# A new hand-written order for every engine of an attention and FFN block kernel

## Chip, cores and metric

One Trainium2 chip, one core (eight are there, one is used). The metric is device time in microseconds (us) of one execution: the median of the runs shown.

## What is computed

Input x has 16 sequences of 512 rows with 256 features (fp32). The reference is

```python
x = x + _layernorm(attn(_layernorm(x)))     # 16 heads of 16, rope on q and k
x = x + _layernorm(ffn(_layernorm(x)))      # 256x256, both operands quantised to fp6 in blocks of 32
# inside attn, with h = layernorm(x) * ln_w + ln_b, q, k, v = h @ w_q, h @ w_kv:
qk = einsum('bhkd,bhqd->bhkq', rope(k), rope(q)) * scale
t = 1.0 + qk + 0.5 * qk * qk
wv = (t / sum(t)) @ v                        # a Taylor softmax, of degree 2
```

## The kernel before

The weights of a Taylor softmax are a polynomial of q and k, so attention is a product of features. A tile is 128 rows of one sequence (NT = 4 tiles a sequence, 64 in all). For each tile the stages are, by engine:

- **Input:** stats_x, moments_x, normalise_x (VectorE, L1326 to L1341) with add_x and rstd_x (GpSimd: an add of one column and a power); turn_z (TensorE transposes), copy_h, high_h (ScalarE), low_h (GpSimd, L1580): fp32 products are made of a high and a low part, three products each (split_product, L644 to L647).
- **q, k, v:** project_v, project_kq (TensorE), copy_v (ScalarE), rope_sin, rope_cos (VectorE, both read PSUM), rope_add (L1367, two SBUF inputs), extend_k (a copy).
- **Features:** products_1 and products_0 (VectorE, L540: products of k's parts, 128x672 and 128x896), products_2 (GpSimd, L540, 128x224), half_turn (GpSimd, L1597), square_k, high_q (ScalarE), low_q (GpSimd, L1585), turn_q (TensorE), copy_q. sum_features (TensorE, L873, 32 matmuls) sums them over a sequence.
- **Once a sequence:** copy_sums, turn_sums (L882), copy_main, rest_terms, constant, rest_matrix (L891, L895), copy_rest.
- **Attention:** select_0 to select_4 (TensorE, L689) with square_0 to square_4 (ScalarE, L1014, L1016), attend (TensorE, L752, L755), copy_quad (ScalarE). SyncE then moves the quad by eight small DMAs (move_quad: sums and heads_out). When a sequence's four quads are there, invert_sums (VectorE, L1405) takes the reciprocals of the denominators, SyncE spreads them by eight DMAs (spread_shares, L626), and normalise_attention (VectorE, L1421) multiplies. Every tile waits there for its own two of the eight. The last two sequences go through TensorE transposes instead (turn_quads, turn_attention).
- **Output of attention:** high_attention, low_attention (GpSimd, L1606), project_out, square_y, add_y, rstd_y, add_attention (VectorE, L1452, reads PSUM).
- **FFN:** centre, square_s (ScalarE), block_maxima, scales, inverse_scales, to_grid (L1470), from_grid (L1478), turn_ffn_input (TensorE), high_ffn_input, low_ffn_input (VectorE, reads PSUM), ffn, add_bias (VectorE, reads PSUM), square_f, add_f, rstd_f, add_ffn (VectorE, L1493), and the store.

Each engine runs its own list in order; semaphores tie the lists together. An instruction that waits holds up all behind it on its engine. The order is written by `stage_steps`: stage s of tile t is issued at step t + LAG[s], corrected by FIRST for the first 12 tiles and by FINAL for the last 16. Within one step the calls in the engine's `step(n)` give the order, so every step of the middle looks alike. `fill` and `drain` (L661) issue idle products of 128x128 with no use for the result: `warm_up` 12 at first, the fills 76 more (88 in all) while the first tiles pass, the drains 96 at the end.

## Time and profile before

| what | value |
|---|---|
| runs | 647.86, 649.33, 651.04 us |
| median | 649.33 us |
| the profiled execution | span 648.2 us; no time of its own is given apart from it |
| TensorE matmul | 624.1 us busy, 96% |
| VectorE | 605.9 us, 93% |
| ScalarE | 569.1 us, 88% |
| GpSimd | 464.6 us, 72% |
| TensorE weight loads | 471.8 us, 73% |
| granted TensorE clock, mean | 0.995 of full speed |
| chain of waits, by engine | VectorE 42%, TensorE 40%, issue 13%, the rest 5% |

PE is TensorE, PEld its weight loads, DVE VectorE, ACT ScalarE, POOL GpSimd, SP SyncE (with q: its queue). Busy time of TensorE is modelled: its matmuls are pipelined. A busy share is a mean over the run; the first 60 us and the last 80 us differ from the middle. In rows of windows the columns are the edges in us, the length, then busy us (instructions) of PE, PEld, DVE, ACT, POOL, the granted clock PEclk (1.00 is full speed), the DMA engines' share and GB/s.

### The profile page before, as it was taken

Reading aid. Unit: us, or ns where it says so; the run is one execution under the profiler, and the core shown is the slowest. Engines: PE = TensorE matmul, PEld = TensorE weight load, DVE = VectorE, ACT = ScalarE, POOL = GpSimd, SP = SyncE. Lnnn points to the kernel's source line nnn. Section 1 sums busy time; section 2 is a strip of 40 time slices with the busy share of each in tenths; the row PEclk is TensorE's granted clock in tenths of the full one; section 3 lists DMA queues with packets and bytes.
Section 4 is the critical chain, followed back from the end, with each engine's and each line's share of the span. In section 5 each row is a group of like instructions: output and inputs, shape, how many; then the busy total and the mean of one; then the engine's idle time right before and its main releaser. Section 6 shows DMA issues by size and latency. Waiting matters only on the chain.

```text
span 648.2 us, 20990 instructions
## 1 busy us (share of the span) xinstructions
PE 624.1 (96%) x6760; PEld 471.8 (73%) x6760; DVE 605.9 (93%) x1424; ACT 569.1 (88%) x1571; POOL 464.6 (72%) x842
## 2 busy tenths in 40 slices
PE   6889999999999999999999999999999999999998
PEld 6676767776777767777776777767767777778887
DVE  5989989999999999999999999999999999996696
ACT  3558899999998999999898999989899999999974
POOL 2675657797778777877787788777777877676364
PEclk9889999999999999999999999999999999999999
DMA  7101121222222232222322222222222212220111
...
DMA packets 52362, 43.54 MB, mean 67 GB/s; under 512 B 7200, under 2 KB 48544, under 8 KB 52256
## 3 DMA queue, kind: packets, MB, share of 16 engines
...
q10 hardware_dynamic: 816, 0.79, 0.4%
...
## 4 chain that ended last, share of the span: by engine, by line
DVE 42%; PE 40%; issue 13%; ACT 2%; POOL 2%; DMA 1%; DVEq 1%; SPq 0%; ACTq 0%; POOLq 0%
DVE kf L540 6%; PE ps_f L689 5%; PE ps_mt L873 5%; DVE xd L1478 4%; DVE kf L1367 4%; PE ps_o L752 4%; DVE z L1340 4%; PE ps_o L755 4%; DVE xs L1452 3%; PE ps_w L644 2%; DVE y L1470 2%; DVE fin L1493 2%; DVE t L1350 2%; DVE fb L1487 2%; PE ps_qk L644 2%
## 5 line engine op out<-in xcount | busy, mean ns | idle before, releaser
L1014 ACT ACTIVATE feat<-ps_f 128x512 f32<-128x512 f32 x256 | 153.1, 604 | 10.9 <-PE ps_f L689 10.2
L689 PE MATMUL ps_f<-qT,selr 128*128 128x512 f32 x320 | 138.0, 436 | 0.6 <-ACT feat L1014 0.6
L540 DVE TENSOR_TENSOR kf<-kf 128x672 f32<-128x672 f32 (+1 forms) x128 | 134.5, 1052 | 2.0
L873 PEld LDWEIGHTS ps_mt<-kf,vp 128*32 128x32 f32 x2048 | 65.5, 109 | 34.1 <-issue 33.3
L1612 POOL TENSOR_TENSOR ve_y<-var_y,epst 128x1 f32<-128x1 f32 x64 | 13.0, 204 | 104.6 <-ACT squares_y L1134 104.5
L873 PE MATMUL ps_mt<-kf,vp 128*32 128x153 f32 x2048 | 78.8, 293 | 0.4 <-ACT rm L1043 0.4
L689 PEld LDWEIGHTS ps_f<-qT,selr 128*128 128x128 f32 x320 | 60.0, 188 | 18.0 <-issue 14.9
L1580 POOL TENSOR_TENSOR hT_l<-hT,hT_h 128x256 fp32r<-128x256 f32 x63 | 56.0, 890 | 23.2 <-ACT hT_h L1079 23.2
L1068 ACT ACTIVATE hT<-ps_tr,small,lnwx 128x128 f32<-128x128 f32 x128 | 51.8, 456 | 20.6 <-PE ps_tr L726 20.5
L752 PE MATMUL ps_o<-feat,main 120*32 120x512 f32 x448 | 59.7, 604 | 0.0
L755 PE MATMUL ps_o<-feat,rm 128*32 128x512 f32 x448 | 58.9, 593 | 0.0
L1585 POOL TENSOR_TENSOR qsp<-kf,qsp 128x256 fp32r<-128x256 f32 x64 | 55.5, 867 | 1.8 <-ACT qsp L1123 1.8
L1606 POOL TENSOR_TENSOR attT_l<-att,attT_h 128x256 fp32r<-128x256 f32 x56 | 49.1, 877 | 9.0 <-ACT attT_h L1054 5.9
L540 POOL TENSOR_TENSOR kf<-kf 128x224 f32<-128x224 f32 x64 | 52.8, 825 | 3.8 <-DVE kf L1374 3.8
L1597 POOL TENSOR_TENSOR kf<-kf 128x128 f32<-128x128 f32 x64 | 53.9, 843 | 0.0
L644 PE MATMUL ps_qk<-wkqv_h,hT_l 128*128 128x512 f32 x126 | 53.9, 428 | 0.0
L645 PE MATMUL ps_qk<-wkqv_l,hT_h 128*128 128x512 f32 x126 | 50.5, 401 | 0.0
L1358 DVE TENSOR_TENSOR t<-ps_qk,sinT 128x512 f32<-128x512 f32 x64 | 43.7, 683 | 5.7 <-PE ps_qk L647 3.5
L1016 ACT ACTIVATE feat<-ps_f,small 128x512 f32<-128x512 f32 x64 | 44.2, 690 | 3.2 <-PE ps_f L689 2.8
L1367 DVE TENSOR_TENSOR kf<-t 128x512 f32<-128x512 f32 x64 | 45.4, 709 | 0.3
L1350 DVE TENSOR_TENSOR t<-ps_qk,cosT 128x512 f32<-128x512 f32 x64 | 42.2, 660 | 2.2 <-PE ps_qk L647 2.2
L1340 DVE TENSOR_SCALAR z<-xa,mv,rs_x 128x256 f32<-128x256 f32 x64 | 41.3, 645 | 2.2 <-POOL rs_x L1616 2.1
...
## 6 DMA issues: line engine op xcount, KB each, us to landing
...
heads_out<-osb SPq DMA_DIRECT2D x224, 32.0 KB, 2.0
shares<-sums SPq DMA_DIRECT2D x112, 64.0 KB
sums<-osb SPq DMA_DIRECT2D x224, 2.0 KB
...
xa<-L_attn_x SPq DMA_DIRECT2D x1, 384.0 KB, 5.5
```

The lines of the kernel that those rows point to most:

```text
L540: return eng.tensor_tensor(dims(row, F_MAIN, [[FW, heads], [HD, NR - 1], [1, HD]]), dims(row, F_LIN, [[FW, heads], [0, NR - 1], [1, HD]]), ...
L644: pe.matmul(out_, xl(c), wh(c), start=c == 0, stop=False)
L689: pe.matmul(ps_f[i % 2][:, :], selr[:, i], queries, start=True, stop=True).then_inc(sel_done, 1)
L752: pe.matmul(ps_o[VW * h:VW * (h + 1), :], main[0:NP, par, quad, VW * h:VW * (h + 1)], feat[0:NP, p2, h], start=True, stop=False, skip_grou ...
L755: mm = pe.matmul(ps_o[VW * h:VW * (h + 1), :], rm[:, par, quad, VW * h:VW * (h + 1)], feat[:, p2, HQ], start=False, stop=True, skip_group_ ...
L873: mm = pe.matmul(ps_mt[qd // 2][VW * h:VW * (h + 1), (qd % 2) * NF:(qd % 2 + 1) * NF], vp[:, s2, qd * HQ + h], kf[:, s2, qd * HQ + h, 0:NF ...
L1014: act.activation(feat[:, p2, i], ps_f[i % 2][:, :], ACT.Square).then_inc(squared, 1)
L1340: dve.tensor_scalar(z[:, t.two], xa[:, t.par, t.tile], mv[:, t.two, 0:1], rs["x"][:, t.two:t.two + 1], ALU.subtract, ALU.mult).then_inc(z_ ...
L1350: dve.tensor_tensor(t1[:].rearrange("p (h d) -> p h d", d=HD), ps_qk[:, :].rearrange("p (h d) -> p h d", d=HD), cos, ALU.mult).then_inc(qk ...
L1367: dve.tensor_tensor(dims(kf[:, t.two, 0, 0:1], F_LIN, [[F_Q - F_LIN, 2], [FW, H], [1, HD]]), t1[:].rearrange("p (a h d) -> p a h d", a=2, ...
L1580: pool.tensor_tensor(hT_l[:, p2], hT[:], hT_h[:, p2].bitcast(F32), ALU.subtract).then_inc(hT_low, 1)
L1585: pool.tensor_tensor(dims(qsp[:, p2], HQ * HD, [[2 * HQ * HD, NQ], [HD, HQ], [1, HD]]), dims(kf[:, p2, 0, 0:1], F_Q, [[HQ * FW, NQ], [FW, ...
```

## The change

The lags are replaced by ORDER: for every engine and stage, the places (slots of that engine's own list) of the first tiles, of a cycle of four tiles (one sequence) that repeats every `pitch` slots, and of the last tiles. TensorE has 58 slots a sequence, ScalarE 75, VectorE 79, GpSimd 52, SyncE 11. Stages once a sequence, of the last eight tiles, and the two loads of x have places of their own (RATE). IDLE is empty: no fill and no drain is issued, warm_up stays. Four waits are added that the new orders need (on s_squared, z_ready, rope_ready, xd_ready).

```diff
--- before.py
+++ after.py
-LAG = {
-    "warm_up": -20, "fill_a": 0, "sum_features": 3, "select_2": 7, "project_v": 1, "drain_b": 16, "select_3": 7,
-    "ffn": 16, "select_4": 7, "turn_q": 3, "turn_sums": 3, "turn_quads": 11, "project_kq": 1, "turn_z": 0,
-    "select_0": 6, "turn_ffn_weight": 7, "project_out": 13, "select_1": 6, "turn_ffn_input": 15, "rest_matrix": 3,
...
+TAIL = 2
+
+
+ORDER = {
+    "tensor": (58, {
+        "attend": ((41, 51, 63, 75, 89, 100, 112, 124, 138, 152, 167, 183, 196, 211, 225, 241, 255, 269, 283, 299, 313,
+            326,), (23, 37, 51, 67,), (676, 689, 705, 718, 733, 747, 763, 778, 791, 805, 821, 836, 850, 860, 875, 891,
+            901, 918, 924,)),
...
+    "vector": (79, {
+        "add_attention": ((142, 156, 167, 187, 209, 229, 250, 271, 290, 310, 334, 352, 370, 389, 409, 429, 450, 469,
+            489, 509, 528, 549, 573, 591, 610, 631, 651, 671, 691, 711, 731, 751, 768, 790, 809, 829, 847, 868, 886,
+            905, 924, 947, 961, 983, 1005, 1025, 1046, 1061, 1081, 1101, 1119, 1137, 1150, 1160, 1174, 1187, 1199, 1211,
+            1224, 1233, 1247, 1257, 1266, 1277,), (), ()),
...
+        "invert_sums": ((116, 166, 247,), (99,), (499, 576, 650, 724, 802, 883, 957, 1038, 1116,)),
...
+        "normalise_attention": ((121, 128, 136, 149, 176, 189, 206, 227, 255, 267, 292, 319, 342, 358, 378, 398, 423,
+            434, 456, 474, 508, 514, 532, 551, 584, 590, 608, 628, 656, 672, 689, 709, 736, 743, 761, 792, 815, 832,
+            852, 872, 894, 913, 935, 950, 973, 991, 1012, 1030, 1052, 1071, 1093, 1107, 1123, 1131, 1136, 1149, 1173,
+            1178, 1195, 1210, 1218, 1232, 1242, 1258,), (), ()),
+        "normalise_x": ((4, 9, 14, 25, 35, 45, 52, 61, 74, 84, 94, 103, 115, 125, 140, 152, 178, 196, 217, 238, 257,
...
+    "gpsimd": (52, {
...
+        "products_2": ((14, 16, 23, 29, 35, 42, 48, 53, 59, 64, 72, 80, 88, 100, 110, 123, 136, 145, 162, 171, 184, 197,
+            210, 224, 236, 249, 263, 277, 288, 301, 314, 331, 341, 352, 363, 378, 390, 402, 417, 428, 443, 454, 469,
+            481, 493, 506, 521, 532, 544, 560, 575, 589, 600, 613, 625, 636, 652, 664, 677, 690, 703, 715, 728, 740,),
+            (), ()),
...
-FIRST = {
-    "fill_a": (-18, -17, -20, -18, -23, -22, -25, -22, 0, 0, 0, 0),
-    "sum_features": (-19, -18, -18, -15, -11, -9, -6, -4, -3, -2, 0, 0),
...
-FINAL = {
-    "sum_features": (0, 0, 0, 0, 0, 0, 0, 0, 0, 0, 0, 0, 0, 3, 9, 13),
...
-EARLY, LATE = 12, 16
-TAIL = 2
-IDLE_FIRST, IDLE_LAST = 8, 12
-
-
-def stage_steps(count):
-
-    plan = {}
-    for stage, lag in LAG.items():
-        steps = plan.setdefault(stage, {})
-        for tile in range(count):
-            step = tile + lag
-            if tile < EARLY:
-                step += FIRST.get(stage, (0,) * EARLY)[tile]
-            elif tile >= count - LATE:
-                step += FINAL.get(stage, (0,) * LATE)[tile - count + LATE]
-            steps.setdefault(step, []).append(tile)
-    return plan
+RATE = {"angles": "once", "bias_mean": "once", "cast_identity": "once", "cast_selection": "once", "centre_bias": "once",
+RATE = {"angles": "once", "bias_mean": "once", "cast_identity": "once", "cast_selection": "once", "centre_bias": "once",
+    "constant": "sequence", "copy_ffn_weight": "once", "copy_main": "sequence", "copy_rest": "sequence", "copy_sums":
...
+IDLE = {"fill": (), "drain": ()}
+
+
+def places(table, count):
+
+    first, cycle, last, pitch = table
+    steps = {}
+    for index in range(count):
+        if index < len(first):
+            place = first[index]
+        elif index >= count - len(last):
+            place = last[index - count + len(last)]
+        else:
+            place = cycle[index % len(cycle)] + pitch * (index // len(cycle))
+        steps[place] = index
+    return steps
 
 
...
@@ -302,10 +424,15 @@
 def sandwich(nc, x, w_q, w_kv, w_o, weight, bias, identity, columns, selection, out):
     NS = x.shape[0]
     TILES = NS * NT
-
-
-    plan = stage_steps(TILES)
-    issued = {stage: 0 for stage in plan}
+    BODY = TILES - NT * TAIL
+    assert NT * TAIL == 8
+    counts = {"tile": TILES, "body": BODY, "tail": TILES - BODY, "sequence": NS, "spread": NS - TAIL, "load": NS - 2, "once": 1}
+
+    plan, issued = {}, {}
+    for engine, (pitch, tables) in ORDER.items():
+        for name, table in tables.items():
+            plan[name] = places(table + (pitch,), counts[RATE.get(name, "tile")])
+            issued[name] = 0
 
     class Tile:
 
@@ -318,42 +445,55 @@
 
     def each(n, name, stage, *args):
 
-        for index in plan[name].get(n, ()):
-            stage(Tile(index), *args)
+        if n in plan[name]:
+            stage(Tile(plan[name][n]), *args)
             issued[name] += 1
 
     def once(n, name, stage):
 
-        for index in plan[name].get(n, ()):
-            if index % NT == NT - 1:
-                stage(Tile(index))
+        if n in plan[name]:
+            index = plan[name][n]
+            stage(Tile(NT * index + NT - 1))
+
+    def body(n, name, stage):
+
+        each(n, name, stage)
+
+    def tail(n, name, stage):
+
+        if n in plan[name]:
+            stage(Tile(plan[name][n] + BODY))
+            issued[name] += 1
+
+    def spread(n, name, stage):
+
+        once(n, name, stage)
+
+    def load(n, name, stage):
+
+        if n in plan[name]:
+            index = plan[name][n]
+            stage(index + 2)
 
     def setup(n, name, stage):
 
-        if n == LAG[name]:
+        if n in plan[name]:
             stage()
 
-    def early(n, name, stage):
-
-        for index in plan[name].get(n, ()):
-            if index < IDLE_FIRST:
-                stage()
-
-    def late(n, name, stage):
-
-        for index in plan[name].get(n, ()):
-            if index >= TILES - IDLE_LAST:
-                stage()
+    def idle(n, name, stage):
+
+        for _ in range(IDLE[name].count(n)):
+            stage()
 
     def wait(eng, sem, count):
 
         if count > 0:
             eng.wait_ge(sem, count)
 
-    def every_step(step):
-
-        used = {n for steps in plan.values() for n in steps}
-        for n in range(min(used), max(used) + 1):
+    def every_step(engine, step):
+
+        last = max(n for name in ORDER[engine][1] for n in plan[name])
+        for n in range(last + 1):
             step(n)
 
     with ExitStack() as ctx:
...
             def step(n):
-                once(n, "invert_sums", spread_shares)
-                each(n, "move_quad", move_quad)
-                each(n, "add_ffn", store)
-                for seq in range(2, NS):
-
-                    if NT * (seq - 1) - 1 in plan["normalise_x"].get(n, ()):
-                        load_stream(seq)
-                    if NT * (seq - 1) - 1 in plan["add_attention"].get(n, ()):
-                        load_again(seq)
+                spread(n, "spread_shares", spread_shares)
+                body(n, "move_quad", move_quad)
+                each(n, "store", store)
+                load(n, "load_stream", load_stream)
+                load(n, "load_again", load_again)
 
             def store(t):
                 sp.wait_ge(fin_ready, t.n)
...
             def fill():
-
-                if issued["attend"] == 0:
-                    idle_products(ps_o, 2)
+                idle_products(ps_o, 2)
 
             def drain():
-
-                if issued["select_4"] == TILES:
-                    pe.wait_ge(squared, CHUNKS * TILES)
-                    idle_products(ps_f[1], 2)
+                pe.wait_ge(squared, CHUNKS * TILES)
+                idle_products(ps_f[1], 2)
 
             def select(t, i):
 
...
             def step(n):
+                idle(n, "fill", fill)
+                idle(n, "drain", drain)
                 setup(n, "warm_up", warm_up)
-                early(n, "fill_a", fill)
                 each(n, "sum_features", sum_features)
                 each(n, "select_2", select, 2)
                 each(n, "project_v", project_v)
-                late(n, "drain_b", drain)
                 each(n, "select_3", select, 3)
                 each(n, "ffn", ffn)
                 each(n, "select_4", select, 4)
                 each(n, "turn_q", turn_q)
                 once(n, "turn_sums", turn_sums)
-                each(n, "turn_quads", turn_quads)
+                tail(n, "turn_quads", turn_quads)
                 each(n, "project_kq", project_kq)
                 each(n, "turn_z", turn_z)
                 each(n, "select_0", select, 0)
...
@@ -1139,6 +1257,7 @@
                 act.wait_ge(xs_ready, t.n)
 
                 wait(act, y8_done, t.n - 2)
+                wait(act, s_squared, t.n - 2)
                 act.activation(c3[:, c2], xs[:, t.four], ACT.Identity, bias=ssum[:, c2:c2 + 1], scale=-float(D)).then_inc(centred, 1)
 
             def square_s(t):
@@ -1332,6 +1451,7 @@
 
             def moments_x(t):
                 dve.wait_ge(stats, t.n)
+                wait(dve, z_ready, t.n - 2)
                 dve.bn_aggr(mv[:, t.two], st[:, t.two]).then_inc(means, 1)
 
             def normalise_x(t):
@@ -1346,6 +1466,7 @@
                 cos = dims(cosT[:], t.tile * HD, [[0, 2 * H], [1, HD]])
                 if t.n == 1:
                     dve.wait_ge(tables_done, 1)
+                wait(dve, rope_ready, t.n - 1)
                 dve.wait_ge(qk_done, t.n)
                 dve.tensor_tensor(t1[:].rearrange("p (h d) -> p h d", d=HD), ps_qk[:, :].rearrange("p (h d) -> p h d", d=HD),
                                   cos, ALU.mult).then_inc(qk_read, 1)
@@ -1354,6 +1475,7 @@
                 sin = dims(sinT[:], t.tile * HD, [[0, 2 * H], [2, 8], [1, 2]])
                 if t.n == 1:
                     dve.wait_ge(tables_done, 1)
+                wait(dve, rope_ready, t.n - 1)
                 dve.wait_ge(qk_done, t.n)
                 dve.tensor_tensor(dims(t2[:], 0, [[HD, 2 * H], [2, 8], [1, 2]]), dims(ps_qk[:, :], 1, [[HD, 2 * H], [2, 8], [-1, 2]]),
                                   sin, ALU.mult).then_inc(qk_read, 1)
@@ -1459,6 +1575,7 @@
 
             def scales(t):
                 dve.wait_ge(amax_done, t.n)
+                wait(dve, xd_ready, t.n - 2)
                 dve.tensor_scalar(sc[:, t.two], amax[:, t.two], 2.0**6 / (D * FP6_MAX), SMALLEST, ALU.mult, ALU.max).then_inc(sc_done, 1)
 
             def inverse_scales(t):
```

In the middle of the run the tables come out as follows (the number is the tile, counted from a multiple of 4). Two tiles of VectorE's list, one tile (before) and two (after) of GpSimd's:

```
VectorE before: rope_cos+1 add_attention-11 rope_add+1 extend_k+1 products_1+1 from_grid-12 normalise_x+3 add_bias-13
    products_0+1 normalise_attention-9 block_maxima-11 scales-11 rope_sin+2 add_ffn-14 inverse_scales-11
    low_ffn_input-12 to_grid-11 stats_x+4 invert_sums-5 moments_x+4 rope_cos+2 add_attention-10 rope_add+2 extend_k+2
    products_1+2 from_grid-11 normalise_x+4 add_bias-12 products_0+2 normalise_attention-8 block_maxima-10 scales-10
    rope_sin+3 add_ffn-13 inverse_scales-10 low_ffn_input-11 to_grid-10 stats_x+5 moments_x+5
VectorE after: rope_cos+1 to_grid-12 low_ffn_input-13 add_attention-11 rope_add+1 normalise_attention-9 extend_k+1
    products_1+1 normalise_x+3 block_maxima-11 products_0+1 from_grid-12 scales-11 add_bias-13 inverse_scales-11
    stats_x+4 to_grid-11 add_ffn-14 rope_sin+2 moments_x+4 rope_cos+2 from_grid-11 stats_x+5 low_ffn_input-12
    rope_add+2 extend_k+2 products_1+2 add_attention-10 products_0+2 block_maxima-10 invert_sums-5 scales-10
    normalise_x+4 inverse_scales-10 add_bias-12 to_grid-10 add_ffn-13 rope_sin+3 normalise_attention-8
GpSimd before: rstd_x+2 add_f-15 rstd_f-15 half_turn+0 products_2+0 low_q+0 add_y-11 add_s-12 rstd_y-11
    low_attention-10 low_h+2 rstd_s-12 add_x+3
GpSimd after: rstd_x+2 products_2+0 half_turn+0 add_s-12 rstd_s-12 low_attention-10 low_q+0 add_y-11 rstd_y-11 low_h+2
    add_x+3 rstd_x+3 products_2+1 half_turn+1 add_s-11 rstd_s-11 add_f-14 rstd_f-14 low_attention-9 low_q+1 low_h+3
    add_y-10 rstd_y-10 products_2+2 low_q+2
```

In VectorE's first slots stats_x of tile 1 now stands ahead of normalise_x of tile 0, the angles behind it, and the first rope_cos and rope_sin stand together, with the scales of the FFN weight after them. On GpSimd the tables stand behind rstd_x of tiles 0 to 2.

## Rows read from the trace of the kernel before

**Rows 1.** Windows of VectorE's reciprocals, first and last of eleven: edges, length, busy us (instructions).

```profile
123.25:160.44 37.19, 36.84 (x399) 27.67 (x388) 36.61 (x87) 34.98 (x97) 29.87 (x52) 1.00 0.23 60
...
495.39:532.61 37.22, 36.49 (x387) 26.92 (x386) 36.63 (x87) 34.58 (x96) 28.87 (x52) 1.00 0.26 74
```

**Rows 2.** Chain of waits, TensorE: start us, us, what; 299.93 to 307.61 is unbroken.

```profile
108.47 0.46 PE ps_mt L882 x4
...
299.93 0.43 PE ps_f L689
...
307.61 1.08 PE ps_mt L873 x32
...
333.70 0.36 PE ps_mt L891 x8
334.06 0.29 PE ps_mt L895 x30
```

**Rows 3.** Groups by form, VectorE, 120 to 560 us: busy us, mean ns, idle before.

```profile
L540 DVE TENSOR_TENSOR kf<-kf 128x896 f32<-128x896 f32 x47 | 58.0, 1234 | 0.0
...
L1478 DVE SCALAR_TENSOR_TENSOR xd<-y,rs_s,sc 128x256 f32<-128x256 fp8e4 x47 | 33.2, 706 | 0.0
...
L1340 DVE TENSOR_SCALAR z<-xa,mv,rs_x 128x256 f32<-128x256 f32 x47 | 32.1, 684 | 0.0
...
L1470 DVE SCALAR_TENSOR_TENSOR y<-c,inv 128x256 fp8e4<-128x256 f32 x48 | 26.6, 555 | 0.0
```

**Rows 4.** Timeline, single VectorE instructions of the same four kinds: start us, us, what.

```profile
46.19 0.41 DVE L1340 TENSOR_SCALAR z<-xa,mv,rs_x 128x256 f32<-128x256 f32 x1
...
47.17 1.09 DVE L540 TENSOR_TENSOR kf<-kf 128x896 f32<-128x896 f32 x1
...
640.09 0.41 DVE L1470 SCALAR_TENSOR_TENSOR y<-c,inv 128x256 fp8e4<-128x256 f32 x1
...
640.54 0.48 DVE L1478 SCALAR_TENSOR_TENSOR xd<-y,rs_s,sc 128x256 f32<-128x256 fp8e4 x1
```

**Rows 5.** Timeline, GpSimd and VectorE at 310 us: start us, us, what.

```profile
310.22 0.76 POOL L1612 TENSOR_TENSOR ve_f<-var_f,epst 128x1 f32<-128x1 f32 x1
...
310.25 0.68 DVE L1367 TENSOR_TENSOR kf<-t 128x512 f32<-128x512 f32 x1
```

**Rows 6.** Timeline of SyncE's queue, chain of waits, and the page's DMA issues (last: us to landing).

```profile
309.39 5.31 SPq L626 DMA_DIRECT2D shares<-sums  x8
...
314.86 0.33 DVE att L1421
...
heads_out<-osb SPq DMA_DIRECT2D x224, 32.0 KB, 2.0
```

**Rows 7.** The start: timeline (in brackets: idle before), chain of waits, the page's DMA issues.

```profile
6.60 0.41 DVE z L1340
...
14.80 0.69 DVE L1358 TENSOR_TENSOR t<-ps_qk,sinT 128x512 f32<-128x512 f32 x1 [2.15 <-POOL sinT L1566]
...
19.19 0.69 DVE L1367 TENSOR_TENSOR kf<-t 128x512 f32<-128x512 f32 x1
...
xa<-L_attn_x SPq DMA_DIRECT2D x1, 384.0 KB, 5.5
```

**Rows 8.** Windows (all work; the last: line L661 alone; PEclk after the brackets) and chain of waits.

```profile
36.60:40.00 3.40, 1.78 (x21) 1.29 (x10) 3.30 (x7) 1.01 (x3) 3.25 (x4) 1.00 0.03 7
40.00:43.40 3.40, 3.08 (x9) 2.51 (x10) 1.75 (x4) 1.62 (x5) 1.34 (x4) 0.50 0.00 0
...
636.00:646.00 10.00, 9.56 (x78) 8.80 (x78) 7.37 (x22) 3.87 (x14) 4.94 (x13) 1.00 0.16 55
...
41.00 0.43 PE ps_qk L644
...
629.50 1.34 PE ps_f L661 x12
...
636.00:646.00 10.00, 6.35 (x53) 6.21 (x54) 1.00 0.16 55
```

449 lines of the change are left out of this document (262 added, 187 removed), and 43 rows, old and new, of the table ORDER.

## The prediction

> **What bounds the kernel now.** I read the busy shares first: TensorE 96%, VectorE 93%, ScalarE 88%, GpSimd 72%. Two engines near full say little, so the next view is by stretches. I cut the middle of the run at the starts of VectorE's once-a-sequence reciprocal; the first and the last of eleven such stretches are in [rows 1]. A sequence of four tiles takes 37.2 us, again and again to 0.03 us, and VectorE is busy for 36.6 of it. ScalarE has 2.2 to 2.6 us to spare, GpSimd over 7. So the middle, 11 x 37.2 = 409 of 648 us, goes at VectorE's pace. TensorE also shows 36.5 to 36.8, but ends of matmuls are modelled, so I take its need from the chain of waits. There the chain stays on TensorE without a break for one whole tile, from the matmul at 299.93 to the end of the attention sums at 307.61 + 1.08 [rows 2]; that tile holds each of TensorE's per-tile stages once and costs 8.76 us. Once a sequence turn_sums adds 0.46 and rest_matrix 0.36 + 0.29. TensorE's need is 4 x 8.76 + 1.11 = 36.15 us a sequence. This is the floor that the change meets: only 1.05 us under the present 37.2.
>
> **What VectorE loses to GpSimd.** The groups by form give the means of the middle [rows 3]; single instructions from places where GpSimd was idle or had just begun give the price without it [rows 4]. Normalising x costs 684 against 410 ns, from_grid 706 against 480, to_grid 555 against 410, products_0 (128x896) 1234 against 1090. Per tile that is 0.274 + 0.226 + 0.145 + 0.144 = 0.79 us, per sequence 3.2. All of these read two SBUF tensors, or are a tensor_scalar within SBUF; the instructions that read PSUM have no such gap. GpSimd can be the one that waits: its one-column add at 310.22 took 0.76 us and ended with the rope_add beside it, which took 0.68 [rows 5].
>
> The Trainium skill (SBUF — State Buffer, Who interferes with whom) says of this that the pair of ports shared by the two engines is an exclusive lock, taken by whichever instruction starts first, and that a VectorE instruction with at most one SBUF input, outside its two-port modes, stays clear of it. The trace agrees as to who is hit, and rows 5 look like such a lock. By its letter a VectorE product that comes second would wait for the whole rest of GpSimd's instruction; what the means above lose, 0.14 to 0.27 us, is less than that, and the sum goes by the means.
>
> **The change, part by part.**
> 1. *The same work in a new order.* Each computing stage of the reference's path is issued as often as before. One lag per stage, plus corrections for the first 12 and last 16 tiles, becomes a slot per stage and tile. The order inside the steady cycle differs on every engine; the depth of the pipeline (how many tiles lie between rope_cos and add_ffn) is the same within one tile.
> 2. *Port conflicts.* GpSimd's half_turn and products_2 trail behind rstd_x and no longer open right beside products_1 of their tile; its four adds and powers are put where VectorE runs the k products, and low_q, low_attention and low_h where VectorE has add_bias, low_ffn_input, stats_x and the ropes. The gain lies between 0 (nothing really moves apart) and 3.2 us a sequence. I walked one tile of the new lists against each other by their waits: low_attention, half_turn and low_q fall beside PSUM reads, products_2 still meets products_0 or add_ffn in some tiles. So not all goes; I take three quarters, 2.4.
> 3. *A wait that comes nearer.* In the order of before, ten instructions (some 5.5 us) lie between invert_sums and the first normalise_attention that needs its shares. Now seven do: scales, normalise_x, inverse_scales, add_bias, to_grid, add_ffn, rope_sin, about 2.9 us. Between them SyncE must issue the shares. As soon as the reciprocal is done, SyncE starts eight issues, at 309.39, 0.66 us each [rows 6]. The first tile needs two of them, and the nearest DMA of that kind (heads_out) lands 2.0 us after its issue: some 2.7 us after the reciprocal at the least; in the old order normalise_attention began at 314.86, 5.5 us after it, and did not wait: that is the most. The stall of VectorE is thus 0 to 2.6 us a sequence; I take 1.3, the middle, since the rows tell only the two ends. Behind the waiting normalise_attention stand rope_cos and the whole next tile, and TensorE's next project_kq waits for that rope.
> 4. *Sum for VectorE.* 36.6 busy - 2.4 + 0.6 (its present idle time, 37.2 - 36.6) + 1.3 = 36.1 us. That is TensorE's floor, 36.15, within the error. With two engines level and ScalarE at 34.6 there will be jitter; I take 0.25 for it: **36.4 us a sequence, 0.8 less than now**. Eleven sequences give -8.8 us, with ends of -12 (at TensorE's floor: 1.05 x 11) and 0. Past the floor, faster VectorE work earns nothing.
> 5. *TensorE's order.* select_0 and select_1 now stand together, and sum_features is followed by project_v rather than select_2. The matmuls are the same and each pays its first-in-group delay as before; 0, with 0.1 us a tile either way.
> 6. *The start.* VectorE now has stats_x of tile 1 ahead of normalise_x of tile 0. That waits for the 384 KB load, issued at 2.1 us and 5.5 long: 7.6. normalise_x started at 6.60 [rows 7], so it and the angles behind it come 1.4 to 2 us later. In return GpSimd's tables no longer stand behind a late rstd_x, and low_v and the weight scales no longer part rope_sin 0 from rope_cos 0: rope_add 0 stood at 19.19 although the tables were there for rope_sin 0 at 14.80. I expect it at 16 to 17. VectorE's work of the ramp remains, so not all of this is kept: -2 us, ends -6 and +3.
> 7. *The idle products are gone.* 76 small matmuls in the start and 96 in the tail. In the tail some stood ahead of real work; the chain crosses a few such groups, the longest of 1.34 us [rows 8], and I estimate the others at as much again: -2.7. But they also kept the array busy. The granted clock fell to its lower level (1.2 of 2.4 GHz) at 40.0, after a stretch in which TensorE was busy 1.78 of 3.4 us; a product of project_kq cost 0.43 us there, and at half the clock that is about twice its usual price. From 636 to 646 TensorE shows 9.56 us, 6.35 of them idle products: without them 3.2 of 10. I expect the clock to fall for the last three or so tiles, at 0.6 us more for ffn (six products, each nearly twice as long) and 0.3 for the transposes: +2.7. Net 0 in the tail, ends -5 and +6. In the start, +0.5 for the first tiles at the low clock, most of it hidden by VectorE's ramp.
> 8. *Added waits* (moments_x on z_ready, the ropes on rope_ready, scales on xd_ready, centre on s_squared) name work that its own engine, or the one it feeds, finished a tile earlier: 0. *Loads with slots of their own* are issued tiles ahead of use: 0.
>
> Sum: -8.8 - 2 + 0.5 + 0 = -10.3, and I add -0.7 for the two sequences on either side of the eleven: **-11 us**. The profiled span is 648.2; the shown runs have a median of 649.33, 1.1 above it, taken as what lies around the span. 649.3 - 11 = **638 us**.
>
> **The rivals.**
> - *A, the forecast:* TensorE and VectorE level at 36.4 us a sequence. 638 us. For: the chain already runs on TensorE for whole tiles. Chance 0.50.
> - *B, better than that:* ramp and tail give their full ends (-6, -5) and the middle reaches 36.2 (-11). 627 us. For: the ramp of before has VectorE waits of over 2 us. Chance 0.20.
> - *C, the lists don't line up on the chip:* engines drift until the same pairs overlap, contention stays at 3.2 us, and VectorE still sets 37.2. Only small start and tail effects: 648 us. Chance 0.13.
> - *D, slower through the shares:* the shares land at the late end, VectorE stalls 2.6 us each sequence, and less than half of the contention goes (-1.4): 36.6 - 1.4 + 0.6 + 2.6 = 38.4, or +1.2 x 11 = +13, less 2 for the start: 660; at the middle of its span 655 us. It decides from the point where stall minus relief passes 0. Against: the relief rests on four rows, all of one sign. Chance 0.12.
> - *E, slower through the clock:* without idle products the low clock holds in the whole ramp and the whole tail. A tile of the ramp has 6 x 0.21 more for project_kq and about as much for the rest, 2.4 us; six tiles and eight tail tiles at about 1.2: +24, less 9 for the middle: 664, or half of it, 656 us. Chance 0.05. [...]
>
> **How the numbers follow.** The likeliest case gives 638. C and the lower part of D close the range above, B below: 626 to 650. About 0.5% (3.2 us) is what a measurement can tell from no change. Faster by more than that: A and B nearly whole, 0.70. Within: C and scraps, 0.14. Slower: D and E, 0.16.
>
> **What would show it.** Right: stretches between reciprocals of 36.2 to 36.6 us; normalise_x below 550 ns and from_grid below 600 in the mean; a chain of waits that stays on TensorE in the middle; a gap before the first normalise_attention of a sequence, ended by the shares' DMA; a few stretches at the low clock in the first 45 and last 10 us. Wrong: a stretch of 37 or more with the same means (C), or with a gap over 2 us at normalise_attention (D), or the low clock over tens of us (E). A stretch much under 36.1 would say that my floor for TensorE is no floor.

## The result, and the profile after

The changed kernel takes 651.87 us (median of 15 runs, 649.15 to 655.88) against 649.88 for the kernel before (15 runs beside it): a ratio of 1.0039, with an interval of 1.0023 to 1.0054. It is slower by some 2.5 us by the ratio (2.0 by the medians); 638 was forecast, and 651.87 lies outside the range of 626 to 650 too. The profiled execution spans 649.8 us against 648.2.

The granted clock of TensorE differs from execution to execution, and the time goes with it. The ten runs of the changed kernel whose mean clock was 0.983 or more took 649.15 to 652.42 us, the five with 0.975 to 0.982 took 652.68 to 655.88. Its fifteen runs have a mean of 0.984; the 29 runs of the kernel before that stood beside start_new have 0.995 and took 647.30 to 651.28. Within each kernel of six runs or more, before and after, a clock lower by 0.01 goes with 2.3 to 5.6 us, mostly about 4. By this (an estimate, from 0.011 of clock) some 4 us of the changed kernel's time go with its lower clock, and at an equal clock it would not be behind. That is a correlation over runs and no proof of a cause: whatever delays TensorE's work may lengthen the run and lower the clock alike.

The page of the kernel after: busy time, and the granted clock in 40 slices.

```profile
PE 613.4 (94%) x6600; PEld 456.2 (70%) x6600; DVE 595.7 (92%) x1424; ACT 570.3 (88%) x1571; POOL 504.7 (78%) x842
...
PEclk9799999999999999999999999999999999999998
...
PE 53%; DVE 17%; issue 10%; ACT 7%; POOL 4%; DMA 4%; SPq 3%; DVEq 0%; ACTq 0%; POOLq 0%
```

VectorE is busy 10 us less, GpSimd 40 us more (504.7 against 464.6). The chain's largest part is now TensorE (53%, before 40%), and it holds 7% of DMA and SyncE's queue, which had 1%: something new.

The reciprocal moves about in the new order, so its starts no longer cut even sequences. I cut instead at the start of rope_cos of each fourth tile. Windows of the kernel after: edges, length, busy us (instructions) of PE, PEld, DVE, ACT, POOL, clock, DMA share, GB/s.

```profile
93.99:130.96 36.97, 35.12 (x372) 23.85 (x368) 34.72 (x72) 33.30 (x87) 25.96 (x41) 1.00 0.18 47
130.96:169.55 38.59, 37.37 (x390) 26.54 (x386) 34.55 (x82) 34.55 (x96) 31.45 (x49) 1.00 0.24 66
169.55:207.48 37.93, 36.77 (x392) 27.20 (x388) 36.30 (x90) 34.30 (x96) 32.44 (x55) 1.00 0.25 66
...
280.54:320.08 39.54, 37.90 (x397) 27.86 (x400) 36.53 (x89) 35.12 (x97) 33.59 (x56) 1.00 0.27 75
...
429.60:466.22 36.62, 36.41 (x385) 27.13 (x385) 33.72 (x81) 34.75 (x97) 31.80 (x53) 1.00 0.29 77
466.22:502.80 36.58, 36.48 (x382) 26.29 (x381) 35.21 (x87) 33.95 (x93) 30.86 (x51) 1.00 0.27 75
502.80:539.30 36.50, 36.47 (x386) 27.42 (x387) 35.65 (x83) 34.84 (x98) 31.59 (x51) 1.00 0.23 61
```

Before, one sequence was as long as the next, 37.2 us [rows 1]. Now there are two halves. The five stretches from 356.90 on last 36.1 to 36.6 us, with TensorE busy to 0.2 us in the last four of them (in the first it has 0.7 us of gaps). The earlier ones last 35.6 to 39.5, with gaps in TensorE and in VectorE. What VectorE waited for between 131 and 360 us (in total, times, longest):

```profile
DVE att L1539 <- DMA shares<-sums: 7.7, 6, 2.5
DVE z L1460 <- POOL rs_x L1731: 1.1, 3, 0.4
DVE xdT_l L1557 <- ACT xdT_h L1210: 1.0, 3, 0.5
```

In the kernel before this list is empty for the same stretch. The longest of the six waits, in the chain of waits of the kernel after (start us, us, what):

```profile
157.24 0.58 SPq L730
...
157.86 1.62 SPq L714
...
159.59 0.68 SPq L755
...
160.31 3.43 DMA shares<-sums
...
163.86 0.09 DVE att L1539
```

and VectorE's end of it, in the timeline of the same kernel (in brackets: idle before):

```profile
157.64 0.89 DVE L1525 RECIPROCAL sums<-sums 64x128 f32<-64x128 f32 x1
...
163.86 0.43 DVE L1539 TENSOR_TENSOR att<-heads_out,shares 128x256 f32<-128x256 f32 x1 [2.52 <-DMA shares<-sums]
```

From the reciprocal's start to the first shares issue pass 1.0 us at the best (here 1.95: SyncE has a store and a load of x in hand). That issue takes 0.7, and the second, with which the first tile is complete, lands 3.43 us after it begins; this one is slow. In five of the six waits SyncE stood ready. In four of them the whole way, from the reciprocal's start to the start of att, took 4.84 to 4.88 us, and the three of these landings that stand in the chain of waits took 2.99 to 3.02 us; in the fifth, with a landing of 3.59, it took 5.45. In the kernel before 6.4 us lay between the reciprocal, at 309.39 - 1.0, and the att of [rows 6]: it had 1.5 us to spare. In the sequences from 384 to 538 us the new order gives 6.7 to 7.5 us, and nothing waits.

Groups by form, VectorE, 120 to 560 us, of the kernel after (busy us, mean ns, idle before), the counterpart of [rows 3]:

```profile
L680 DVE TENSOR_TENSOR kf<-kf 128x896 f32<-128x896 f32 x47 | 56.5, 1203 | 0.0
L680 DVE TENSOR_TENSOR kf<-kf 128x672 f32<-128x672 f32 x47 | 45.5, 968 | 1.0
...
L1610 DVE SCALAR_TENSOR_TENSOR fin<-fb,rs_f,xs 128x256 f32<-128x256 f32 x46 | 25.9, 563 | 0.2
L1460 DVE TENSOR_SCALAR z<-xa,mv,rs_x 128x256 f32<-128x256 f32 x47 | 25.5, 542 | 2.1 <-POOL rs_x L1731 1.8
L1595 DVE SCALAR_TENSOR_TENSOR xd<-y,rs_s,sc 128x256 f32<-128x256 fp8e4 x47 | 25.3, 539 | 0.6 <-DVE y L1587 0.5
...
L1587 DVE SCALAR_TENSOR_TENSOR y<-c,inv 128x256 fp8e4<-128x256 f32 x47 | 20.9, 445 | 0.0
```

The four that I had watched fell: 142, 167, 110 and 31 ns a tile, 0.45 us. But products_1 rose from 861 to 968 and add_ffn (fin) from 475 to 563, with smaller rises in rope_cos, rope_add, extend_k and low_ffn_input. With what rest_terms and constant gained, once a sequence (0.6 us together), 1.1 us a sequence is left. And GpSimd pays: its products_2 rose from 798 to 961 ns, rstd_x from 551 to 733.

Where the time went, told by TensorE's work: I counted its matmuls but for the idle ones, each at its usual duration, and asked when either kernel had done the same share. The changed one was 1.6 us ahead at 87 us, 1.2 behind at 136, 3.8 at 211, 5.5 at 378, then 2.7 at 575 and 1.4 at the end. So it wins 1.6 in the start, loses 7.1 up to 378, wins back 2.8 in the late middle and 1.3 in the tail. The first of these is the least certain. Counted the same way, other kernels below with the same order up to 87 us stand elsewhere there: drain_back some 3.6 us ahead (clock 0.89 in its first 30 us), ends_new some 2.9 behind (0.71).

### The profile page after: what moved, and what is told of

Read it like the earlier page. It is cut to its first block, busy times and chain, and to the rows that moved or that the text cites. A ratio compares the mean times of both kernels' runs of the same rounds, so it can differ in the third digit from the quotient of the medians.

```text
span 649.8 us, 20921 instructions
## 1 busy us (share of the span) xinstructions
PE 613.4 (94%) x6600; PEld 456.2 (70%) x6600; DVE 595.7 (92%) x1424; ACT 570.3 (88%) x1571; POOL 504.7 (78%) x842
## 4 chain that ended last, share of the span: by engine, by line
PE 53%; DVE 17%; issue 10%; ACT 7%; POOL 4%; DMA 4%; SPq 3%; DVEq 0%; ACTq 0%; POOLq 0%
PE ps_f L814 7%; PE ps_mt L993 6%; PE ps_o L875 5%; PE ps_o L878 4%; PE ps_qk L773 4%; DMA shares<-sums 3%; PE ps_qk L774 3%; PE ps_qk L776 3%; DVE kf L680 3%; PE ps_w L773 3%; PE ps_w L776 3%; PE ps_w L774 3%; PE ps_tr L838 3%; PE ps_tr L773 2%; ACT feat L1132 2%
## 5 line engine op out<-in xcount | busy, mean ns | idle before, releaser
L1132 ACT ACTIVATE feat<-ps_f 128x512 f32<-128x512 f32 x256 | 143.7, 599 | 1.0 <-PE ps_f L814 0.9
L680 DVE TENSOR_TENSOR kf<-kf 128x896 f32<-128x896 f32 (+1 forms) x128 | 139.5, 1094 | 1.4
L814 PE MATMUL ps_f<-qT,selr 128*128 128x512 f32 x320 | 117.2, 427 | 4.2 <-ACT feat L1132 3.4
L680 POOL TENSOR_TENSOR kf<-kf 128x224 f32<-128x224 f32 x64 | 62.3, 974 | 8.3 <-DVE kf L1496 8.3
L1702 POOL TENSOR_TENSOR qsp<-kf,qsp 128x256 fp32r<-128x256 f32 x64 | 60.1, 939 | 9.5 <-ACT qsp L1241 9.2
L1697 POOL TENSOR_TENSOR hT_l<-hT,hT_h 128x256 fp32r<-128x256 f32 x63 | 52.9, 839 | 16.9 <-ACT hT_h L1197 16.5
L814 PEld LDWEIGHTS ps_f<-qT,selr 128*128 128x128 f32 x320 | 52.1, 189 | 15.4 <-issue 7.9
L1731 POOL TENSOR_TENSOR rs_x<-ve_x,mhalf 128x1 f32<-128x1 f32 x64 | 46.8, 731 | 3.5
L1714 POOL TENSOR_TENSOR kf<-kf 128x128 f32<-128x128 f32 x64 | 38.5, 602 | 11.4 <-DVE kf L1489 11.3
L1731 POOL TENSOR_TENSOR rs_s<-ve_s,mhalf 128x1 f32<-128x1 f32 x64 | 41.8, 654 | 5.0
```

What stands on the lines that cost most here:

```text
L680: return eng.tensor_tensor(dims(row, F_MAIN, [[FW, heads], [HD, NR - 1], [1, HD]]), dims(row, F_LIN, [[FW, heads], [0, NR - 1], [1, HD]]), ...
L814: pe.matmul(ps_f[i % 2][:, :], selr[:, i], queries, start=True, stop=True).then_inc(sel_done, 1)
L1132: act.activation(feat[:, p2, i], ps_f[i % 2][:, :], ACT.Square).then_inc(squared, 1)
L1697: pool.tensor_tensor(hT_l[:, p2], hT[:], hT_h[:, p2].bitcast(F32), ALU.subtract).then_inc(hT_low, 1)
L1702: pool.tensor_tensor(dims(qsp[:, p2], HQ * HD, [[2 * HQ * HD, NQ], [HD, HQ], [1, HD]]), dims(kf[:, p2, 0, 0:1], F_Q, [[HQ * FW, NQ], [FW, ...
L1731: pool.tensor_tensor(rs[c][:, t.two:t.two + 1], ve[c][:, t.two:t.two + 1], mhalf[:], ALU.pow).then_inc(rstd[c], 1)
```

## The experiments

Sixteen kernels. Most edits are made in the tables of places; their diffs show what the lists then say.

**Which stretch of the order costs the time?** Three kernels that join the two orders at a reciprocal, and one for the idle products.

```diff
 start_new:  new order of every engine, up to reciprocal 2 (118 us)
-            then the rest of the new order
+            then what is left, in the old order
 late_new:   old order up to reciprocal 7 (308 us), then the new one
 ends_new:   new up to reciprocal 2, old up to 7, new to the end
 idle_back:
-IDLE = {"fill": (), "drain": ()}
+IDLE = {"fill": (16 places in the start), "drain": (17 in the tail)}
```

start_new:

> The changed kernel's order on every engine up to the second reciprocal of the sums (118 us), the order of the kernel before for all that is left, its idle products of the tail with it. Theory O (what an order gains or loses lies in the stretch in which it stands): the changed kernel was 4.3 us ahead at that point, so 649.9 - 4.3 = 645.6, stretches of 37.2 from then on. Rival G (a lead is given back, since the old middle sets its own pace from fixed points): 649 to 650.

It took 650.76 us, 1.0027 (1.0008 to 1.0046) of before. Its stretches are 37.3 us from the join on, but the 4.3 us are not there: they were largely the reciprocal's own earlier place. Counted by TensorE's work, 2.8 us of lead at 87 us are 1.1 by 165 us, and stay that in this profile, while the timed runs show no gain. Rival G, in the main: the start of the new order is worth a microsecond at most. Like the changed kernel it issues no idle products in the start; no_fill below tells what that alone costs in the old order (1.2 us).

late_new:

> The order of the kernel before up to the seventh reciprocal (about 314 us), then the changed kernel's to the end, without idle products in the tail. Theory O: from there the changed kernel gained 7.2 us by the thirteenth reciprocal (36.0 against 37.2 us a sequence) and gave 2.2 back by the next: 649.9 - 5 = 645. Rival C (its gain there only made up for time lost before, as a pipeline that refills): within 1.5 us of before, 650, with stretches of 37 us. The clock of the last 9 us stays at its lower level in either.

651.9 us, 1.0034 (1.0015 to 1.0054). Counted by TensorE's work it loses 4.6 us between 303 and 378 us, with two waits for the shares among them (2.7 us); from 357 on its stretches are 36.1 to 36.7 us, as in the changed kernel, and win 2.7 back. The late new order is faster than the old (36.5 against 37.2), but what leads into it costs as much. Rival C is nearer than theory O.

ends_new:

> The changed kernel's order up to the second reciprocal and again from the seventh on, the order of the kernel before for the five sequences between. Theory O: both gains at once, 649.9 - 4.3 - 5 = 640.6, so that the 11 us which the changed kernel loses between 118 and 280 us are shown to be that stretch's order alone. Rivals G and C: 649 to 651. If only one of the two gains holds: 645.

651.4 us, 1.0027 (1.0000 to 1.0053). So my reading of the reciprocals' starts was wrong, not only my theory: a marker that the change moves does not measure progress. The clock takes part here too. Four of its twelve runs had 0.990 to 0.992 and took 647.88 to 648.71 us, where the eleven runs of the kernel before at 0.992 took 650.03 to 651.28; its other eight had less clock and took 649.48 to 656.17. Something of the two gains is there, some 2 us at an equal clock, and the 640.6 are not. Its profiled run is the slowest one: the clock fell even in the middle, 0.53 from 316 to 322 us, where the two orders meet and TensorE had been busy for 4.3 of the 6 us before.

idle_back:

> The changed kernel with the idle products of the kernel before put back, each ahead of the same tensor stage as there (16 calls in the start, 17 in the tail). Theory O (the order of the middle lost the time, the clock little): the granted clock at its lower level in the last 9 us goes away, worth at most 2 us, and the idle products stand in front of real work for about as much; 651 us, within 1.5 us of the changed kernel. Rival K (the clock of start and tail lost it): 4 us or more below the changed kernel, 647 or less.

655.13 us, 1.0091 (1.0067 to 1.0114): 3.3 us slower than the changed kernel, with a mean clock of 0.996 in its runs. Theory K falls: the clock is back and the time is not. The 17 calls of the tail are all that stood ahead of TensorE's work there; the other 7 of the kernel before (28 of its 96 records in the trace) come after its last piece of work, and start_new and no_fill go without them as well. A product leaves two records, and the 16 calls of the start leave 64, not the 76 that the text before the result and the prediction name: warm_up alone has 24. The chain of waits of idle_back shows idle products on the path (L885 is their line; start us, us):

```profile
23.32 0.44 PE ps_o L885 x4
...
27.36 0.89 PE ps_o L885 x8
...
31.23 1.34 PE ps_o L885 x12
...
36.66 0.45 PE ps_o L885 x4
```

**Are the waits for the shares the cause?** Two kernels, one each way.

```diff
 shares_early, VectorE's list, sequence 6 (likewise 0, 2 to 5 and 7, by 1 to 3 places)
-add_attention 22, products_0 34, block_maxima 22, invert_sums 6, scales 22
+add_attention 22, invert_sums 6, products_0 34, block_maxima 22, scales 22
 SyncE's list, sequence 2
-load_stream, spread_shares, move_quad
+spread_shares, load_stream, move_quad
```

> The changed kernel with the reciprocal of the sums one to three places earlier in VectorE's list for sequences 0 and 2 to 7, the first normalise_attention of sequences 0 and 2 one and two places later, and SyncE's shares of sequence 2 ahead of its load of x. Theory S (the six waits for the shares, 7.7 us of idle VectorE in sequences 2 to 7, are what made the middle slower): these waits go, and those stretches come down toward the later ones, which TensorE sets at 36.6 us: 5 to 7 us less than the changed kernel, 645 to 647. Rival V (VectorE's irregular order and its relief that was too small set the pace there; the waits only take up idle time it had anyway): within 2 us of the changed kernel, 650 to 652.

It took **646.23 us**, 0.9943 (0.9921 to 0.9966) of before: 5.6 us less than the changed kernel, and less than both. The waits for the shares of 0.2 us and more are down from 10.1 us in the whole run to 1.2. Stretches of shares_early:

```profile
242.20:278.40 36.20, 35.84 (x382) 27.15 (x382) 34.88 (x85) 33.84 (x95) 32.23 (x53) 1.00 0.25 70
278.40:314.82 36.42, 35.91 (x380) 27.14 (x372) 35.18 (x88) 33.93 (x94) 32.27 (x53) 1.00 0.30 79
314.82:351.05 36.23, 36.23 (x385) 27.47 (x384) 34.89 (x87) 35.00 (x98) 32.37 (x52) 1.00 0.25 67
```

The stretch that lasted 39.54 now lasts 36.42, with the same work in it. Theory S holds. The runs have the same mean clock as those of the changed kernel (0.985 and 0.984), so the clock has no part in this difference. Of 8.9 us of waits taken away, 5.6 came back as time.

```diff
 shares_late_old, VectorE's step of the kernel before
-                once(n, "invert_sums", invert_sums)
 ...
                 each(n, "extend_k", extend_k)
+                once(n, "invert_sums", invert_sums)
```

> The kernel before with one line moved: VectorE's reciprocal of the sums five places later, behind extend_k, some 2.2 us nearer to the normalise_attention that needs its shares. The distance falls from 5.4 to about 3.2 us, and the trace of the changed kernel shows that 4.85 are needed. Theory S: a wait of about 1.65 us at each first normalise_attention, paid in full, since VectorE bounds this kernel: 37.2 + 1.6 = 38.8 us a sequence, 650 + 12 x 1.6 = 669 us. Rival V: the wait is there, but the work behind it catches up: under 660.

658.67 us, 1.0143 (1.0111 to 1.0174). Its waits of VectorE from 120 to 560 us:

```profile
DVE att L1421 <- DMA shares<-sums: 10.5, 12, 1.2
```

The wait is 0.87 us each, and the sequence goes from 37.2 to 38.0: here, where VectorE bounds every sequence, nearly the whole price is paid, 0.8 for 0.87. The expectation had the distance wrong (from start to start it fell from 6.4 to 4.0 us, against 4.85 needed; I had set a distance from the reciprocal's end beside one from its start), not the rule.

**What is TensorE's own pace?** Four kernels take work off the engines beside it.

```diff
 floor_old, floor_new
-                k_products(dve, t, half * H // 2, H // 2 - half * HG)
+                k_products(dve, t, half * H // 2, 1 if half == 0 and t.n > 2 else H // 2 - half * HG)
 quiet_old (relaxed_new: these two and the cut above, on top of shares_early), from the third tile on
-                k_products(pool, t, H - HG, HG)
+                one product of 16 columns
-                half_turn over [FW, H]
+                half_turn over [FW, 1]
```

> The kernel before with products_0 of one head in place of eight from the third tile on (the features of seven heads are stale, so that part of the result is left out); VectorE has about 1 us less a tile, 4 a sequence, and TensorE's work is the same. It shows what a sequence costs when TensorE alone sets it. If the floor of the prediction holds: stretches of 36.15 us. If the late stretches of the changed kernel are the floor: 36.5 to 36.6.

> The same cut of products_0 in the changed kernel. Its late stretches stay at 36.5 to 36.6 us if they are TensorE's own pace. Under theory S the early ones (sequences 2 to 7) keep a wait for the shares and stay 0.5 to 1 us above the late ones; under rival V they come down to the same 36.6, since VectorE has time to spare. The run would end near 640 us.

> The kernel before with GpSimd's products_2 cut to one product of 16 columns and half_turn to one head of 16 from the third tile on (those features are stale, that part of the result is left out); VectorE's work is the same. If GpSimd's instructions are what lengthens VectorE's: normalise_x falls from 645 to below 450 ns in the mean, from_grid below 520, and VectorE saves about 2 us a sequence; the stretches come down from 37.2 to TensorE's 35.6 us of floor_old, some 630 us in all. If VectorE is long for another reason: means and stretches stay, 648.

> shares_early with VectorE's products_0 cut to one head, and GpSimd's products_2 and half_turn cut as in quiet_old, from the third tile on (those features are stale, that part of the result is left out). Neither engine can hold TensorE up any more by being late with its work. If TensorE's new order itself costs more than the old one: all stretches between 36.2 and 36.6 us, where the old order showed 35.6 in floor_old and quiet_old; about 638 us. If it was waiting in small pieces for the other two: 35.6 to 35.8 us, about 631.

They took 629.69, 646.55, 629.32 and 638.98 us, one run each. A stretch of the windows of floor_old:

```profile
235.97:271.61 35.64, 35.64 (x392) 27.01 (x388) 33.10 (x87) 34.18 (x96) 27.26 (x53) 1.00 0.27 77
```

of quiet_old:

```profile
271.42:307.06 35.64, 35.64 (x396) 27.02 (x388) 34.42 (x87) 34.19 (x97) 27.17 (x53) 1.00 0.31 77
```

of floor_new, an early and a late one:

```profile
130.66:168.78 38.12, 36.52 (x382) 26.26 (x375) 31.72 (x82) 33.78 (x93) 27.82 (x48) 1.00 0.24 67
...
497.02:533.59 36.57, 36.25 (x383) 27.07 (x384) 33.12 (x83) 34.42 (x97) 27.12 (x49) 1.00 0.23 60
```

and of relaxed_new:

```profile
417.42:453.78 36.36, 36.36 (x386) 27.35 (x385) 30.25 (x81) 34.83 (x98) 26.71 (x54) 1.00 0.29 80
453.78:489.78 36.00, 35.93 (x381) 26.07 (x381) 30.81 (x88) 33.74 (x92) 25.41 (x51) 1.00 0.27 76
```

In the old order TensorE alone needs 35.64 us a sequence, twice over, by two different cuts. In the new order the last five stretches are 36.3 us in floor_new and 36.2 in relaxed_new, where VectorE has 5 us to spare and TensorE still shows no gap over 0.2 us. So in the new order TensorE takes about 0.6 us a sequence more. One part of it can be seen: project_v's first product, which now stands behind sum_features. Groups by form, 360 to 520 us, of floor_old, relaxed_new and relaxed_mix (below), which has the old TensorE order among the other engines' new ones:

```profile
L644 PE MATMUL ps_tr<-wkqv_h,hT_l 128*128 128x256 f32 x36 | 9.2, 279 | 0.0
...
L867 PE MATMUL ps_tr<-wkqv_h,hT_l 128*128 128x256 f32 x34 | 10.2, 324 | 0.0
...
L867 PE MATMUL ps_tr<-wkqv_h,hT_l 128*128 128x256 f32 x32 | 8.4, 286 | 0.0
```

It takes 45 ns more, 8 times a sequence: 0.36 us. It follows TensorE's order and not its neighbours. project_kq's counterpart gives back some 0.1 (424 to 408 ns). Where the rest comes from is open; ScalarE, whose new order no cut relieves, is not ruled out for it.

floor_new was expected near 640 and took 646.55. Its six early stretches are 36.9 us in the mean, the late ones 36.3, and its longest early row keeps 38.12 us: VectorE had a microsecond less to do each tile and the sequence stayed long, because the wait for the shares (2.9 us there) does not care how busy VectorE is. That is theory S once more.

**Does the old TensorE order help in the new surroundings?**

```diff
 tensor_mix (from shares_early) and relaxed_mix (from relaxed_new), TensorE's list
-sum_features 41, project_v 43, select_2 37, select_3 37, ffn 28, select_4 37
+sum_features 41, select_2 37, project_v 43, select_3 37, ffn 28, select_4 37
-select_0 38, select_1 38, project_out 31
+select_0 38, project_out 31, select_1 38
```

> shares_early with TensorE's stages in the kernel before's order within each tile, from tile 14 to 59 but one (sum_features, select_2, project_v, select_3, and so on; select_0 and select_1 apart again). floor_old repeated at 35.6 us, floor_new at 36.3, both with TensorE never idle. If TensorE's order alone makes that difference: late stretches of 35.9 to 36.2, 640 to 643 us. If the other engines' new orders no longer fit (they finish a tile's pieces in the order that the new TensorE list asks for): TensorE waits, stretches above 37, over 650.

> The same cuts in tensor_mix, which stood at 37 to 41 us a sequence. If its waits were for VectorE and GpSimd only: 35.6 to 36 us a sequence now, near 632. If they are for ScalarE, whose own order and 34.6 us of work a sequence are not touched: still above 37, over 650.

676.93 us, 1.0421 (1.0398 to 1.0444), and 672.33 for relaxed_mix. TensorE's waits in tensor_mix, 120 to 560 us:

```profile
PE ps_f L908 <- ACT feat L1226: 8.3, 15, 1.5
PE ps_mt L1096 <- ACT mts L1238: 5.1, 7, 1.9
```

and in relaxed_mix, with VectorE and GpSimd relieved:

```profile
PE ps_f L908 <- ACT feat L1226: 6.7, 11, 1.5
PE ps_mt L1096 <- ACT mts L1238: 5.1, 7, 1.9
```

The longest are for ScalarE, whose list still reads out TensorE's products in the other order. These two rows are 13.4 and 11.8 us of the 31 and 33 that the mixes lose against shares_early and relaxed_new; the rest was not traced. The 0.6 us can't be had by TensorE's list alone; a list that suits all was not tried.

**What does GpSimd cost VectorE?** quiet_old above answers for the whole (groups by form of quiet_old, 120 to 560 us):

```profile
L1478 DVE SCALAR_TENSOR_TENSOR xd<-y,rs_s,sc 128x256 f32<-128x256 fp8e4 x49 | 23.4, 478 | 0.0
...
L1470 DVE SCALAR_TENSOR_TENSOR y<-c,inv 128x256 fp8e4<-128x256 f32 x49 | 20.6, 419 | 0.1
```

from_grid drops from 706 to 478 ns (480 in [rows 4]), to_grid from 555 to 419 (410), normalise_x from 684 to 408 (410). GpSimd is what lengthens them. products_0 does not drop (1234 to 1253), so that kernel gives no support to the 1090 that the prediction set against it.

```diff
 bias_first, VectorE's step of the kernel before
+                each(n, "add_bias", add_bias)
                 each(n, "from_grid", from_grid)
                 each(n, "normalise_x", normalise_x)
 ...
-                each(n, "add_bias", add_bias)
```

> The kernel before with one line moved: VectorE's add_bias (which reads PSUM) ahead of from_grid instead of behind normalise_x, so that it runs beside the end of GpSimd's half_turn and products_2. If a small shift of this kind gives relief: from_grid and normalise_x lose some 100 ns of their means between them, 0.1 us a tile, 0.4 a sequence: 645. If the overlap only moves on to the next of VectorE's instructions: 650 within 1 us.

653.34 us, 1.0049 (1.0032 to 1.0065). Groups by form, as above:

```profile
L540 DVE TENSOR_TENSOR kf<-kf 128x896 f32<-128x896 f32 x48 | 71.1, 1481 | 0.0
...
L1340 DVE TENSOR_SCALAR z<-xa,mv,rs_x 128x256 f32<-128x256 f32 x47 | 32.7, 695 | 0.0
...
L1493 DVE SCALAR_TENSOR_TENSOR fin<-fb,rs_f,xs 128x256 f32<-128x256 f32 x45 | 27.2, 605 | 0.0
...
L1478 DVE SCALAR_TENSOR_TENSOR xd<-y,rs_s,sc 128x256 f32<-128x256 fp8e4 x47 | 22.3, 475 | 0.0
```

from_grid lost all its 231 ns, and products_0 took on 247 and add_ffn 130. The overlap moved on and grew. The Trainium skill (SBUF — State Buffer, Who interferes with whom) has this as an exclusive lock of the pair of ports; the trace agrees in kind: a conflict that leaves one instruction comes back in others, here with more than it was (231 ns gone, 377 new).

**The idle products, apart.**

```diff
 no_idle (kernel before): fill and drain left out;  no_fill: fill alone left out
 drain_back (kernel after): the 17 drain calls of idle_back alone
```

> The kernel before's order on every engine, without its idle products in start and tail. Putting them back into the changed kernel cost 3.2 us. If they cost in either order: about 3 us less than before, 647. If they pay in the order of before, by holding the clock up (rival K): slower than before by 2 us or more, with the lower clock in the last 9 us and in more of the start. The forecast's own term said 0 in the tail and 0.5 lost in the start.

> The kernel before's order without the idle products of the start, those of the tail kept. Leaving out both made it 1.8 us slower. If the tail's are what pays (by the clock of the last 9 us): equal to before within 0.7 us, 650. If the start's are: slower by all of the 1.8, 652.

> The changed kernel with the idle products of the tail alone put back, 17 calls. Putting back both cost 3.2 us. If the tail's cost it, since in this order they stand in front of work that is ready: 655. If the start's did: 652 or a little less, as the changed kernel.

no_idle took 651.93 us, 1.0035 (1.0019 to 1.0050); no_fill 651.42, 1.0018 (1.0005 to 1.0031); drain_back 652.74, 1.0047 (1.0030 to 1.0064). In the old order leaving them out loses 1.8 us; the start's alone lose 1.2, and the difference between the two is within what these runs can tell. In the new order putting back the tail's adds 0.9 to the changed kernel, within what these runs can tell, and the start's another 2.4. The end of no_idle (windows as above):

```profile
640.00:648.50 8.50, 2.83 (x12) 2.13 (x11) 2.66 (x7) 1.29 (x5) 1.48 (x4) 0.50 0.15 51
```

The clock is at its lower level from 640.0 to the end; TensorE was busy for 1.59 of the 3.4 us before it fell, and for a third of the time after. The Trainium skill (TensorE: Matmul & The Clock Gate, Part 1) says that an array left idle goes back to 1.2 GHz. The trace agrees in the direction, but this array was half busy when the clock fell. What these last microseconds cost is small: 0.5 us lie between the medians of no_fill and no_idle, whose intervals overlap.

## Why the prediction was wrong, step by step

- *The bound.* Right: VectorE set 37.2 us a sequence. floor_old takes only work of VectorE away and gets 35.64, quiet_old only GpSimd's, which lengthens VectorE's, and gets the same.
- *TensorE's need, 36.15.* Wrong by 0.5: the old order's need is 35.64, and the unbroken tile of the chain, 8.76 us, held 0.13 more than a tile needs. What that is was not looked at.
- *Step 1, "the order inside the steady cycle".* **This failed first.** There is no steady cycle in the new lists of VectorE, GpSimd and ScalarE: they name a place for nearly every tile. I walked one sequence and multiplied by eleven. The list of VectorE shown ahead of the prediction is that of sequence 6 (reciprocal at 314.85 us) and of no other. The late half came out at 36.1 to 36.6 us, within the 36.2 to 36.6 that I named, nearly; the six sequences before it did not (37.7 in the mean).
- *Step 2, contention.* Right in kind, wrong in size: 2.4 us a sequence foreseen, 1.1 measured. I summed over the four instructions that had been hit and not over those that would be: the four gave 0.45 us a tile, products_1 and add_ffn took 0.2 of it back, and bias_first shows how whole a conflict is passed on. Over half of the 1.1 is rest_terms and constant, once a sequence, which I had not counted. The 40 us on GpSimd I had not foreseen.
- *Step 3, the shares.* The mechanism is the one that happened, even the size (7.7 us in six sequences, 1.3 each). That size is luck: 1.3 was the middle between two ends, the other sequences of the middle do not wait at all, and a mean over all eleven is 0.7. Its least way of 2.7 us after the reciprocal's end, taken from heads_out landing 2.0 us after its issue [rows 6], is 3.9 (4.85 from its start): the shares take 3.0 to land, and up to 3.6. And the distance is no constant: without the waits it is 3.5 to 7.5 us from start to start between 120 and 560 us. This wait is paid by the run, in shares_late_old by 0.8 us for 0.87, in shares_early by 5.6 for 8.9.
- *Step 4, the sum.* 36.6 - 1.1 + 0.6 + 1.3 = 37.4 for the sequences that wait (37.7 measured, 130.96 to 356.90); TensorE's 36.6 for those that don't. With the measured terms the same sum comes to within 0.3 us of the early sequences. The twelve stretches from 93.99 to 539.30 us take 445.3 us; the same tiles took 444.7 before, where -9.5 was foreseen.
- *Step 5, TensorE's order, 0.* Wrong: about +0.6 us a sequence (relaxed_new against floor_old). It is most of what caps the late half at 36.1 to 36.6, where the old order needs 35.64. About 0.36 of it is at project_v's first product behind sum_features, a change that this step had named and set at 0; the rest was not settled.
- *Step 6, the start, -2.* No run shows it. The profile stands 1.6 us ahead at 87 us, but profiles of the same start stand between 3.6 ahead and 2.9 behind there, and start_new, timed, gains nothing. Of its parts, normalise_x 0 came 1.4 us later, as told; the first rope_add at 18.38 us in place of 16 to 17 (timeline of the kernel after):

```profile
7.98 0.40 DVE L1460 TENSOR_SCALAR z<-xa,mv,rs_x 128x256 f32<-128x256 f32 x1
...
18.38 0.69 DVE L1489 TENSOR_TENSOR kf<-t 128x512 f32<-128x512 f32 x1
```

- *Step 7, the idle products, about 0.* Two large terms of opposite sign, and what is left of them depends on the order: the products earn 1.8 us in the old order and would cost 3.3 in the new one, where they would stand in front of ready work. To put them back is no remedy. But the clock was not free: it is at its lower level for some 17 us of the profiled run, before for 7, and by the runs' own clocks some 4 us go with that (the estimate above). Rival E falls as it was priced, since the low clock holds neither in the whole ramp nor in the whole tail; the slowest runs, 655.5 to 655.9 us at a clock of 0.975 to 0.977, come up to its lower figure all the same. The clock fell where it was expected (windows of the kernel after):

```profile
15.32:22.14 6.82, 4.31 (x13) 3.38 (x14) 4.70 (x10) 3.80 (x12) 5.25 (x12) 0.50 0.00 0
25.56:28.97 3.41, 3.41 (x36) 2.49 (x28) 3.31 (x6) 0.69 (x2) 2.20 (x4) 0.50 0.51 150
643.37:649.00 5.63, 1.62 (x6) 1.33 (x6) 1.39 (x3) 0.51 (x2) 1.41 (x4) 0.50 0.21 70
```

- *Step 8, the added waits, 0.* Right: none of them shows among the waits, but for 0.2 us at moments_x.
- *The rivals.* D is what happened, in half of the sequences: the shares' wait against a relief below half of the contention. It had 0.12. Its price there, 1.2 us a sequence, against 0.5 measured (37.7 to 37.2). Where the wait was absent a sequence took 36.5, near to A; the six sequences with it, and the lower clock, ate what that gained. Its point of decision, "where stall minus relief passes 0", was the right question.
- *The signs.* Nearly all that were to show a right forecast came: normalise_x 542 and from_grid 539 ns, a chain mostly on TensorE, the gap ended by the shares' DMA, low clock at both ends. None of them tells a gain from a loss; the one that does, the length of each stretch, held for some five of twelve.
- *What is accounted for.* 13.9 us lie between the forecast and 651.87. The waits for the shares are 5.6 of them, shown by shares_early. About 4 go with the clock, by the estimate above. The 2 of the start and what the tail did are not shown by any run.
